# Even and odd halves of the spectral stage in one bank with the 1x1 layer's halves, layer norm by the statistics instruction, and another order in the front

## What is computed

```
x = x + L0(gn(x))     # per-image mixed 3x3 depthwise convolution, then a 1x1 layer (32 -> 32)
x = x + L1(gn(x))
```

```
hidden = depthwise3x3(w_hidden @ x)             # 32 -> 192 channels
q, k, v = split(hidden, 3)                      # 64 channels each
out = irfft2(rfft2(patch8(q)) * rfft2(patch8(k)))   # circular convolution of 8x8 patches
out = (out - mean over 64 channels) / sqrt(var over 64 channels + 1e-5)
out = out * norm_w + norm_b
y = w_out @ (v * out)                           # 64 -> 32 channels
```

## Time and profile before

| | |
|---|---|
| median of 3 runs | 3041.64 us (3037.79 to 3047.04) |
| profiled execution, its own time | 3043.07 us |
| span of its trace | 3041.0 us |
| mean granted TensorE clock | 0.961 of full speed |
| TensorE busy | 2679.8 us (88% of the span) |
| ScalarE busy | 2219.4 us (73%) |
| VectorE busy | 2039.6 us (67%) |
| GpSimd busy | 574.6 us (19%) |

### The profile page before, as it was taken

One profiled execution on the slowest core, in us unless ns is written; L12 is line 12 of the kernel. 1 busy time (PEld: TensorE's weight loads), 2 busy tenths in 40 slices (PEclk: granted clock), 3 DMA queues, 4 the chain that ended last, 5 costly groups with the idle time before them and its releaser, 6 DMA issues.

```text
span 3041.0 us, 74966 instructions
## 1 busy us (share of the span) xinstructions
PE 2679.8 (88%) x28031; PEld 1676.5 (55%) x28031; DVE 2039.6 (67%) x3469; ACT 2219.4 (73%) x4445; POOL 574.6 (19%) x307
## 2 busy tenths in 40 slices
PE   2777777779999999999999999999999999999998
PEld 1222222226666666666666666666666666666665
DVE  7666666644767676666666667676666767676766
ACT  2455555558878787878787878787787878787885
POOL 4000000010222222222222222222222222222222
PEclk9898888879999999999999999999999999999999
DMA  9899999982222222223222222222222222222221
GB/s 190 203 283 276 287 271 270 270 212 66 59 59 58 59 58 59 69 63 72 62 69 63 68 59 58 59 58 59 59 58 59 58 59 58 59 58 59 58 58 42
DMA packets 43485, 313.88 MB, mean 103 GB/s; under 512 B 12913, under 2 KB 13050, under 8 KB 29658
## 3 DMA queue, kind: packets, MB, share of 16 engines
q1 hardware_dynamic: 43082, 308.58, 40.7%
HBM read 206.81 MB, written 101.72 MB: 101 GB/s over the span
## 4 chain that ended last, share of the span: by engine, by line
PE 60%; DVE 14%; ACT 9%; DMA 8%; issue 8%; SPq 1%; ACTq 0%; DVEq 0%; POOL 0%; POOLq 0%
PE bank L614 15%; PE bank L696 14%; PE bank L676 8%; DMA arena<-x_in 8%; PE bank L627 6%; PE bank L687 5%; PE bank L599 5%; PE bank L636 4%; DVE arena L1110 3%; ACT arena L862 3%; PE bank L562 2%; DVE arena L1130 2%; ACT arena L764 2%; DVE arena L1194 1%; DVE arena L1124 1%
## 5 line engine op out<-in xcount | busy, mean ns | idle before, releaser
L862 ACT ACTIVATE arena<-bank 64x256 f32<-64x256 f32 x2048 | 773.2, 378 | 141.0 <-PE bank L687 122.3
L486 POOL TENSOR_TENSOR arena<-arena 128x8 f32<-128x8 f32 x256 | 515.5, 2014 | 1833.8 <-DVE arena L1132 1833.7
L614 PE MATMUL bank<-arena 128*64 128x512 f16 x4608 | 715.2, 401 | 45.3 <-issue 45.3
L805 ACT ACTIVATE arena<-bank 100x512 f32<-100x512 f32 x1024 | 585.5, 639 | 105.5 <-PE bank L599 103.2
L1194 DVE TENSOR_TENSOR arena<-bank,arena 128x512 f32<-128x512 f32 x512 | 354.5, 692 | 455.4 <-ACT arena L862 410.4
L696 PE MATMUL bank<-arena 100*128 100x128 f32 x4096 | 590.0, 286 | 0.0
L696 PEld LDWEIGHTS bank<-arena 100*128 100x128 f32 x4096 | 495.8, 191 | 82.5 <-issue 82.5
L599 PEld LDWEIGHTS bank<-arena 128*64 128x64 f16 (+1 forms) x8192 | 340.4, 106 | 254.3 <-ACT arena L805 48.8
L599 PE MATMUL bank<-arena 128*64 128x128 f16 (+1 forms) x8192 | 414.4, 223 | 21.4 <-ACT arena L805 17.9
L562 PE MATMUL bank<-arena 128*32 128x512 f32 x3072 | 413.1, 679 | 4.7 <-DVE arena L986 4.0
L821 ACT ACTIVATE arena<-bank,arena 128x256 f32<-128x256 f32 x512 | 261.3, 561 | 138.5 <-PE bank L627 135.8
(11 more groups left out here) (122 smaller groups left out, 2133.1 us busy)
## 6 DMA issues: line engine op xcount, KB each, us to landing
arena<-xn_d SPq DMA_DIRECT2D x128, 536.2 KB, 8.9
xn_d<-arena SPq DMA_DIRECT2D x130, 260.0 KB, 14.1
arena<-x_in SPq DMA_DIRECT2D x64, 512.0 KB, 25.6
x_d<-arena SPq DMA_DIRECT2D x64, 512.0 KB, 14.7
arena<-x_d SPq DMA_DIRECT2D x128, 256.0 KB, 4.9
out<-arena SPq DMA_DIRECT2D x128, 256.0 KB, 4.4
arena<-x_in SPq DMA_DIRECT2D x16, 2047.9 KB, 26.9
arena<-spectra_in SPq DMA_DIRECT2D x1, 1152.0 KB
```

Source lines behind the costliest of these rows:

```text
L486: pool.tensor_tensor(tiny["rstd"][:, slot], tiny["var_eps"][:, slot], powers, ALU.pow).then_inc(s_root, 1)
L614: mm = pe.matmul(v_banks[chunk % 3][64 * s:64 * s + 64, :], v_w[:, 64 * tap:64 * tap + 64], at(xs[half], row * WP + 32 * k + dx, [32 * WP, ...
L805: act.activation(h_rows[0:WIN, :, first:first + 4], banks[g % ring][0:WIN, :].rearrange("p (i c) -> p c i", i=4), ACT.Copy).then_inc(s_h_r ...
L862: ins = act.activation(at(q_sb[n % 4][64 * to:64 * to + 64, :], 128 * half, [256, 2], [1, 128]), src, ACT.Copy)
```

## The change

**Spectral part.** k is computed like q on 64 columns: its two parts (`part`) of an even and an odd channel (`par`) go to the two halves of the partitions. k has three banks instead of two. q is computed for eight channels at a time and copied by one instruction of 128x512. The inverse runs once for eight channels: eight matmuls of 64 rows and 64 columns, four at a time in the quarters of the array, adding up over the two parts, into two banks; it is copied out by two instructions per sixteen channels. The first chunk of v moves from the front to the end of the spectral part, ahead of the last inverse.

**Layer norm.** Channel sums, squares and their sums go. In their place four `bn_stats` per piece (32 per unit), each over 64 channels of two neighbouring pixels, 128 elements in turn, whose even and odd statistics are those of the two pixels. `variance` and `centre` read them directly.

**Order in the front.** On VectorE, `scale` of a piece now stands right behind `variance` and `centre` of the same piece, and the window behind it. On TensorE the groups are spread as 2, then 4, 5, 5, 5, 4, 4, 3 beside the seven chunks of v.

```diff
-            def channel_sums(u, i):
...
-            def variance(u, p):
-
-                dve.wait_ge(s_squared, 8 * u + p + 1)
...
+            def pixel_stats(u, p):
+
+                if p == 0:
+                    dve.wait_ge(s_y_ready, 8 * (u + 1))
+                for s in range(2):
+                    for j in range(0, 4, 2):
+                        first = 24 * (p % 2) + 12 * s + 3 * j
+                        ins = dve.bn_stats(T["pixel_stats"][:, first:first + 6], at(Y, 2048 * s + 4 * p + j, [32, 64], [1, 2]))
+                ins.then_inc(s_pixel_stats, 1)
...
-                negative_mean(tail)
-                centre(tail, 0)
-                centre(tail, 1)
+                for p in range(2):
+                    pixel_stats(tail, p)
+                    variance(tail, p)
+                    centre(tail, p)
+                scale(tail, 0)
                 windows()
...
+                scale(tail, 1)
                 for p in range(8):
-                    if p + 3 < 8:
-                        centre(tail, p + 3)
-                    if p + 2 < 8:
-                        variance(tail, p + 2)
-                    if p + 1 < 8:
-                        scale(tail, p + 1)
-                    if p in (0, 1, 2, 4):
-                        windows()
+                    if p < 6:
+                        pixel_stats(tail, p + 2)
                     if p < 7 or u is None:
                         gate(tail, p // 2, p % 2)
+                    if p < 6:
+                        variance(tail, p + 2)
+                        centre(tail, p + 2)
                     if p in (2, 4, 6):
                         residual(tail, p // 2 - 1)
+                    if p < 6:
+                        scale(tail, p + 2)
+                    windows()
...
-                v_chunk(tail, v_half, 0, 0, 6, hidden)
-                v_chunk(tail, v_half, 0, 1, 6, hidden)
-                turn(tail, 0, 0)
...
+                hidden(2)
+                for k in range(4):
+                    v_chunk(tail, v_half, k, 1, (4, 5, 4, 3)[k], hidden)
+                    if k > 0:
+                        project(tail, k - 1)
                     turn(tail, k, 0)
                     if k < 3:
-                        v_chunk(tail, v_half, k + 1, 0, 3, hidden)
+                        v_chunk(tail, v_half, k + 1, 0, (5, 5, 4)[k], hidden)
...
-                        mm = pe.matmul(banks[2 + n % 2][:, 128 * i:128 * i + 128], G_k[0:WIN, 128 * ch:128 * ch + 128],
...
+                                mm = pe.matmul(k_banks[n % 3][64 * par:64 * par + 64, 256 * part + 128 * pair:256 * part + 128 * pair + 128],
+                                               G_k[0:WIN, 128 * ch + 64 * part:128 * ch + 64 * part + 64],
...
+                def inverse_octet(m):
+                    for part in range(2):
+                        for par in range(2):
+                            for lam in range(2):
+                                mm = pe.matmul(i_banks[par][64 * lam:64 * lam + 64, 256 * (m % 2):256 * (m % 2) + 256],
+                                               small["inverse"][64 * par:64 * par + 64, 64 * part:64 * part + 64],
+                                               at(prod[m % 2][64 * par:64 * par + 64, :], 256 * part + 64 * lam, [512, 2], [128, 2], [1, 64]),
+                                               start=part == 0, stop=part == 1)
...
+                v_chunk(u, half, 0, 0, 0, None, lambda: inverse_inputs(7))
+                inverse_octet(7)
...
-                    for half in range(2):
-                        src = banks[n % 2][64 * half:64 * half + 64, 0:256].rearrange("p (i j) -> p i j", i=2)
-                        for to in range(2):
-                            ins = act.activation(at(q_sb[n % 4][64 * to:64 * to + 64, :], 128 * half, [256, 2], [1, 128]), src, ACT.Copy)
-                    ins.then_inc(s_q_copied, 1)
+                    act.activation(q_sb[m % 2], banks[m % 2], ACT.Copy).then_inc(s_q_copied, 1)
```

More of the change, by code:

```diff
@@ L68, in constants @@
     a = 2 * np.pi * ((u[:, None] * u[None, :] + v[:, None] * v[None, :]) % 8) / 8
-    out["inverse"] = (np.concatenate([np.cos(a) + np.sin(a), np.sin(a) - np.cos(a)]) / 64).astype(np.float32)
+    both = np.concatenate([np.cos(a) + np.sin(a), np.sin(a) - np.cos(a)], axis=1) / 64
+    out["inverse"] = np.tile(both, (2, 1)).astype(np.float32)
     return out
@@ L282, in build @@
         G_k = take(64 * 128)
-        squares = take(1024)
-        q_sb = [take(512) for _ in range(4)]
-        prod = [take(512) for _ in range(2)]
+        q_sb = [take(512) for _ in range(2)]
+        prod = [take(1024) for _ in range(2)]
         xs = [take(HALF * WP, f16) for _ in range(2)]
@@ L601, in hidden_group, with v_chunk @@
                 mm.then_inc(s_hidden_mm, 1)
-            def v_chunk(u, half, k, jr, groups, between):
+            def v_chunk(u, half, k, jr, groups, between, before_last=None):
                 chunk = 2 * k + jr
-                if chunk == 1:
-                    pe.wait_ge(s_y_ready, 8 * (u + 1))
+                if chunk == 0:
+                    pe.wait_ge(s_prod_ready, 16 * u + 14)
+                if chunk in (1, 2):
+                    pe.wait_ge(s_y_ready, 8 * (u + 1) - 2 + chunk)
                 if chunk > 2:
@@ L610, in v_chunk @@
                 for tap in range(9):
+                    if tap == 8 and before_last is not None:
+                        before_last()
                     dy, dx = tap // 3, tap % 3
@@ L700, in spectral @@
+                q_octet(0)
+                if tail is not None:
+                    turn(tail, 3, 1)
+                for m in range(8):
+                    if m < 7:
+                        q_octet(m + 1)
+                    if m == 0:
+                        k_quad(0)
+                    else:
+                        k_quad(2 * m, m - 1)
+                        inverse_octet(m - 1)
+                    k_quad(2 * m + 1)
+                    if m == 0 and tail is not None:
                         project(tail, 3)
-                    if n > 0:
-                        inverse(n - 1)
@@ L710, in _ @@
                     front(u, half, u - 1)
-                    spectral(u, u - 1)
+                    spectral(u, half, u - 1)
             front(LAST, 1, LAST - 1)
-            spectral(LAST, LAST - 1)
+            spectral(LAST, 1, LAST - 1)
             front(None, 0, LAST)
@@ L1091, in _ @@
             Y4 = Y.rearrange("p (s c j) -> p s c j", s=2, j=32)
-            sq4 = [squares[:, 512 * i:512 * i + 512].rearrange("p (s c j) -> p s c j", s=2, j=4) for i in range(2)]
-            by_chan = lambda a: a.rearrange("p s c j -> p s j c")
             over = lambda a: a.rearrange("p (s j) -> p s j", s=2).unsqueeze(2).broadcast_to([128, 2, 64, 4])
-            pair = lambda a: a.rearrange("p (s j) -> p s j", s=2)
             def window(u, half, r, b=None):
@@ L1134, in scale @@
+                dve.tensor_tensor(piece, piece, mean, ALU.subtract).then_inc(s_y_centred, 1)
             def scale(u, p):
```

168 lines of the change are left out of this document (66 added, 102 removed).

## The result

| | before | after |
|---|---|---|
| median | 3044.34 us (4 runs, 3037.79 to 3052.52) | 3299.43 us (4 runs, 3297.49 to 3303.49) |
| ratio | | 1.084, 95% interval 1.081 to 1.087 |
| span of the trace | 3041.0 us | 3301.7 us |
| mean granted TensorE clock | 0.961 | 0.933 |

The change makes the kernel 255 us slower. The forecast was 3163 us, 121 slower, with 3265 as its upper end: the sign is right, the size less than half, and the result outside the range.

What follows compares the result with a forecast made beforehand. TensorE bounded the kernel before; a new front loop through GpSimd's root outweighs the spectral gain. Mean 3.9 us per unit longer over 31 units, 121 us onto 3043.07, less 1.4 for the median, gives 3163 us; range 3095 to 3265.

Steps and rivals of the forecast that it cites:

- The steady flow of the spectral part: Spectral part: eight channels in 3.8 us instead of 4.2, so 3.4 us per unit less.
- the two changes of form: Spectral part: matmuls switch between 64 and 128 columns twice in eight channels, 0.15 us each, 0.30 against 0.72 before.
- the sum: Whole unit: front 7.3 us longer, spectral part 2.7 less, so 4.6 longer, or 3.9 on the mean.
- both rivals on the quarters: Spectral part's inverse: quarters in two turns, 3383 us (chance 0.05); or at the skill's row-tile speed, 3230 us (no chance given).
- The loop: Front: transpose, gate, variance, root, multiplication, window, last group, next transpose take 6.25 us, 7.2 with the output layer; 7.8 added.
- The fast rival: Front: chain from transpose to window is shorter than TensorE's own 3.7 to 4.6 us; near 2855 us, chance 0.08.
- The root takes 2.0 us on GpSimd, whatever else changes: Front: fixed root length, with 2.30 us from variance start to multiplication start.
- VectorE's round: Front, r = 3 and 4: VectorE's own work with the root takes 4.9 us per piece, 1.2 and 0.8 late.
- a rival with 0.11: Front: the new waits lower TensorE's clock in most fronts, up to 70 us more, 3233 us; chance 0.11.
- The two pieces ahead of the loop: Front, r = 3 and 4: bound by VectorE at 4.9 us per piece, 1.2 and 0.8 us late.
- the jump: Units behind a jump: VectorE works on during TensorE's 3.2 us, so the unit is 3.2 us longer, not 4.6.
- the sum for the first piece: Start of front: copy-out, statistics 0.84, variance, root, multiplication take 5.45 us; TensorE arrives after 3.5 and waits 1.65.

Runs made afterwards that it cites:

- the copy alone: Changed kernel plus a copy of the eight means between variance and subtraction, read by nobody; the subtraction still reads strided means: 3165.17 us, 1.037.
- The run with TensorE kept at work: Changed kernel plus eight pairs of idle 512-column matmuls on TensorE ahead of hidden groups 20, 24 and 28: 3220.89 us, 1.0571.
- the root a piece later: Changed kernel with only VectorE's front order altered: variance and centring of piece p+2, then multiplication of p+1, window, gate, residual: 2910.36 us, 0.954.

## Why the prediction was right in sign and wrong in size

**Right.** The steady flow of the spectral part: 3.85 in eight channels (3.8 forecast), q goes over into k without a gap, the two changes of form cost 0.17 and 0.18 (1.03 and 1.06 against 0.86 and 0.88) where the sum had 0.15 each, and the quarters run side by side; both rivals on the quarters fall. Statistics: four in 0.86, so 0.21 each as forecast. The loop, its links and its place: gate 1.80 behind the transposes (1577.75 to 1579.55), variance 0.60 behind the gate, window 0.61 behind the multiplication. TensorE waits at the window copy, VectorE for GpSimd. The fast rival, in which the loop doesn't close, fell: no kernel in which the multiplication stays as close behind its own variance as in the change came below the kernel before.

**Wrong: "The root takes 2.0 us on GpSimd, whatever else changes".** It takes 2.35 on average and 2.4 to 2.5 in the loop; variance to multiplication is 2.74 (1580.15 to 1582.89), not 2.30. The row of before held the reason, which I did not look for: there a multiplication of 0.69 (L1139, of the piece ahead) was already under way when the root began, and the root's length was made of both. I priced the new subtraction at 0.61 because it stood under the root's cover. It lasts 1.07, and carries the root with it. 0.44 longer in the five intervals per unit that the loop or VectorE's round sets, times 31, would be 68 us. That the root's length hangs on this was shown by the copy alone (-134 us, though that root is also 0.4 shorter than the one I had assumed, and the clock gains too). The link from window to group is 0.70 where 0.62 stood in the sum, which is some 7 us more.

**Wrong: the clock was left out of the number.** I had seen in the earlier trace rows that a lightly used stretch is followed by 3.4 us at 1.2 GHz, and priced it at 0 to 70 as a rival with 0.11. The run with TensorE kept at work puts it at 78 us, and at the high clock the kernel would stand at about 3221. With waits of 2.4 to 3.0 us in three places of each front, the low clock was the likely case, not the rival. I had also looked for its cost in the wrong place. Output layer and transposes run inside the loop, so half rate there lengthens the loop one to one (8.72 against 7.62 in the fronts shown). But on the mean the loop's three intervals lose only 0.6 us per unit to it (22.4 against 21.8); 1.5 are lost in the interval behind the loop (5.9 against 4.4), which has no wait to cover it, and 0.6 in the spectral part.

**What the other 58 us are.** With TensorE kept at work a unit takes 78.4 us on average and before it took 72.6: 5.7 more, where the sum had 3.9. Four terms of the sum make up the 1.8 between, as far as the traces' means show. The loop's three intervals are 7.4, 7.6 and 6.8, so 2.1 more than the 6.25, 7.2 and 6.25 of the sum. The two pieces ahead of the loop were priced too high: they come 0.8 us late together (4.5 and 5.3 against 4.2 and 4.8 with the root a piece later), not 1.2 and 0.8; these 1.2 go the other way. That is luck: without it the miss would be 36 us larger, and it is why the links' 68 and 7 us don't show in full. The head of a front, up to its first transpose, is 3.9 shorter than before, where the sum, with what it took off for the jump, had 4.6. And the spectral part is 2.4 shorter, not 2.7. In the sum for the first piece, besides, the terms named make 5.1, not 5.45; the trace shows 5.9 in a front without a jump ahead of it and 5.1 in one behind a jump.

**The range.** Its bounds came from the statistics, the form and the clock, and the first two were hardly off; the root, the longest link, had no bound at all.

## What to carry to other kernels

When a step is moved so that an engine waits for it, follow what is queued behind the waiting instruction: here one window copy behind one multiplication turned GpSimd's 2.4 us into TensorE's. A duration read beside other work is a duration in that company; look at what overlapped it before reusing it. And where TensorE is to wait as it does here (three times 2.4 to 3.0 us in a front), put the low clock behind the waits into the number, not in the tail, and look first at the work that no wait covers.

Parts of a change that lose singly may win together, and the other way round: the new spectral part and the new layer norm were worth 138 us together here, and only VectorE's order of statement hid it.

## What the runs showed of the hardware

GpSimd's root of 128x8 has no fixed length. DVE and POOL on their timelines, in the kernel before:

```profile
1576.61 0.69 DVE L1139 TENSOR_TENSOR arena<-arena 128x512 f32<-128x512 f32 x1
```
```profile
1576.78 2.01 POOL L486 TENSOR_TENSOR arena<-arena 128x8 f32<-128x8 f32 x1 [2.23 <-DVE arena L1132]
```

in the changed kernel:

```profile
1580.23 1.12 DVE L1126 TENSOR_TENSOR arena<-arena 128x512 f32<-128x512 f32 x1
...
1580.40 2.46 POOL L483 TENSOR_TENSOR arena<-arena 128x8 f32<-128x8 f32 x1 [4.33 <-DVE arena L1119]
```

and with the copy alone:

```profile
1607.88 1.11 DVE L1128 TENSOR_TENSOR arena<-arena 128x512 f32<-128x512 f32 x1
```
```profile
1607.85 1.64 POOL L484 TENSOR_TENSOR arena<-arena 128x8 f32<-128x8 f32 x1 [3.16 <-DVE arena L1120]
```

In the first two the VectorE instruction has started 0.17 before the root, and the root ends 1.49 and 1.51 after that instruction's end (1577.30 to 1578.79, 1581.35 to 1582.86). It is so in all 256 roots of the kernel before (1.49 behind the end, 2.01 long) and in most of the changed kernel's. In the third the root starts 0.03 ahead and takes 1.64 from its own start, and the subtraction beside it is not held up either (1.11 here, 1.09 on the mean). It looks as if GpSimd waited for the end of the VectorE instruction in flight; the runs show the times, not the mechanism. With the root a piece later some last 3.49, with VectorE at work without a break beside them; there the end of the first instruction in flight does not explain the length.

Four quarters of 64 rows and 64 columns, in fp32, cost one another nothing that shows: 1.03 us for the inverse of eight channels, against the 0.86 and 0.15 for a change of form that I had reckoned. By the Trainium skill ("TensorE: Matmul & The Clock Gate", Measured speedup vs the span model) four row tiles of 32 rows reach 3.07 times the speed of one. Carried over to these quarters, which are two row tiles by two column tiles, that made an estimate of 1.12 without the change of form; the measurement decides, and it lies below.

A subtraction of 128x512 whose second operand is read at a stride of three words takes 1.07 us, also where GpSimd does nothing (1.07 in the run without roots); with the same values side by side 0.72. The statistics instruction on pairs of pixels at a stride shows no such price: 0.21 each.
